# Where three small setup pieces stand among the first LSTM cells

## The chip, the core and the metric

The kernel runs on one core of a Trainium2 chip. The metric is device time in microseconds, from the launch's start to its end, as the median of several runs. Profiles come from one profiled execution: TensorE is PE (its weight loads PEld), VectorE is DVE, ScalarE is ACT, GpSimd is POOL, and SP issues DMAs. Each engine works through its own instruction list in order; semaphores tie the lists together.

## The reference

The input is `x` (16 batches, 512 nodes, 128 features) and an adjacency matrix of 512 x 512. Four graph layers follow one another, each with a residual sum and a layer norm:

```python
x = _layernorm(x + L0(x, adj))   # graph convolutions, order 2
x = _layernorm(x + L1(x, adj))   # normalized adjacency, two linear maps with batch norm
x = _layernorm(x + L2(x, adj))   # two graph convolutions, then LSTMs over windows of 1 to 4 nodes
x = _layernorm(x + L3(x, adj))   # 8 Euler steps of a diffusion
```

L3 is, for `t` in 8 steps,

```python
h = h + dt * (alph * 0.5 * (adj @ h - h) + h @ w_eff - h + x0)
```

Because it is linear in `h` and `x0`, the kernel writes the 8 steps as a polynomial: powers of the node matrix times powers of the feature matrix, plus a constant (`euler_bias`) that comes from the bias `fc_in_b` and needs to be made only once.

## The kernel before

The first half of the program (L0 and L1) ends at about 190 us. The second half handles L2 and L3 for 8 groups of two batches each. It is software-pipelined: in step `g` the engines run the 11 LSTM cells of group `g`, the front of L2 (turn, gather, weight) for group `g + 1`, and L3 of groups `g - 1` and `g - 2`.

The order is written out by hand. For each engine there is a table with one list for each of the 11 cells; `step` issues cell `c` and then the pieces that list `c` names (line 1252 and on). The cells are, by index: 0 and 1 the windows of one node (one for each batch), 2 and 3 the windows of two nodes (first and second time step), 4 to 6 those of three, 7 to 10 those of four. A cell on TensorE is the input matmuls (`wih`, three for each gate) and, from the second time step on, the recurrent ones (`whh`, L1860, L1861 and L1864), which wait for the state that VectorE writes. While the state is being made (ScalarE's gates L1433, VectorE's products L1585 to L1606, ScalarE's tanh L1436), TensorE works on the pieces of the list. The state of one cell group is the input of the next: cell 2 waits for the outputs of cells 0 and 1.

The first step (`ONCE_` tables) and the second (`NEXT_` tables) also carry the setup of L3, once. Three pieces of it matter here; all lead to `euler_bias`:

- `offset` (L2052): nine matmuls with 6 columns of weights into PSUM, then VectorE's copy (L1819) to `bc`. It needs the last of `fc` (`f_kept`).
- `lift`: twelve matmuls of the third power with 6 columns of weights (through the helper at L141 to L143, `pow_h,vpad_h`), eight small ones (L2063, L2064), then ScalarE's copy (L1557) to `vec_t`. It needs the low part of the last `second` piece (`p_lo`, VectorE L1748).
- `bias` (L2072): four matmuls of both, over 6 rows, then VectorE's copy (L1823) to `euler_bias`. L3's first transpose `x3t_0` (L1921) waits for that copy in the second step, since it uses the same PSUM banks.

Other names that occur: `gather0` and `gather1` are the products with the adjacency (`adj_h,node_h`), followed by ScalarE's cast (L1488) and VectorE's low part (L1643); `weight0` (L1900) and `weight1` (`gat_h,wg_parts`) use these; `hlate` (L2003) transposes the LSTM's result of the step before; `turn_0` (L1876) transposes the next group's input; `mix_0` to `mix_7` (L1810) are VectorE's sums for the coefficients of L3; the suffix is the batch of the pair. Every fp32 operand is kept as a high and a low part (`_h`, `_l`), which makes three matmuls of each product.

Of the kernel before, what the change touches and what calls it, by code (L numbers as in the profile page):

```python
# [54 lines left out]
def program(nc, x_t, adj_n, adj_t, nv1_t, nv2, l0_w, l0_b, w1_t, bn1, w2_t, bn2, wg, bg0, bg1,  # L55
# [4 lines left out]
    with ExitStack() as whole:  # L60
# [3 lines left out]
        def sb(name, shape, dt=F32):  # L64
# [25 lines left out]
                   w1_t, bn1, w2_t, bn2, eye, wg, wih_t, whh_t, bih, bhh, adj_h, adj_l, wih_h, wih_l, whh_h, whh_l,  # L90
                   wg_h, wg_l, gate_bias, row_sums, x1_dram, o2_dram, raw, xt, x1, small, small_in, steps)
        second_half(nc, sem, psum, wg_parts, banks, ident, exponent, scale2, shift2, adj_h, adj_l, wih_h, wih_l, whh_h, whh_l,
                    wg_h, wg_l, gate_bias, row_sums, x1_dram, o2_dram, x2_dram, raw, xt, x1, small, steps, out)

# [845 lines left out]
def second_half(nc, sem, psum, wg_parts, banks, ident, exponent, scale2, shift2, adj_h, adj_l, wih_h, wih_l, whh_h, whh_l,  # L940
# [8 lines left out]
    with ExitStack() as ctx:  # L949
# [215 lines left out]
        def outputs(c, source, ones, twos):  # L1165
# [9 lines left out]
            if p == 3:  # L1175
# [11 lines left out]
        FILL_ACT = [[], ["x3norm_0", "x3split_0", "evens_h"], ["x3t_0", "norm_0"],  # L1187
                    ["power1_0", "power2_0", "evens_l", "out_0", "gather0_0"], ["rest_h", "coefs0_0", "prep_1", "weight0_0", "x3norm_1"],
                    ["coefs1_0", "x3split_1", "rest_l"], ["gather1_0", "x3t_1", "norm_1"], ["power1_1", "out_1", "power2_1"],
                    ["input_0", "gather0_1"], ["weight0_1", "coefs0_1"],  # L1190
                    ["coefs1_1", "gather1_1", "ahead_0", "inner_0", "input_1", "inner_1"]]
# [38 lines left out]
        START_SP = ["norm_0", "norm_1"]  # L1230

        ONCE_PE = [[], ["turn_0", "first_3", "square"], ["cube", "second_0"], ["gather0_0", "fourth", "second_1"],
                   ["weight0_0", "fc_0"], ["turn_1", "fc_1"], ["gather1_0", "fc_2", "second_2"], ["weight1_0"],
                   ["gather0_1"], ["weight0_1", "second_3"], ["gather1_1", "offset", "weight1_1"]]
        ONCE_ACT = [["prep_0"], ["first_3"], ["norm_0", "evens_h", "second_0"], ["evens_l", "gather0_0", "second_1"],
                    ["rest_h", "prep_1", "weight0_0"], ["rest_l"], ["gather1_0", "second_2"], ["norm_1"],
                    ["input_0", "gather0_1"], ["weight0_1", "second_3"], ["gather1_1", "ahead_0", "input_1"]]
        ONCE_DVE = [[], ["turn_0", "first_3", "square"], ["cube", "second_0"], ["gather0_0", "fourth", "second_1"],
                    ["weight0_0", "fc_0"], ["turn_1", "fc_1"], ["gather1_0", "fc_2", "second_2", "mix_0"],
                    ["weight1_0", "mix_1"], ["gather0_1", "input_0", "mix_2"], ["weight0_1", "second_3", "mix_3"],  # L1240
                    ["gather1_1", "offset", "weight1_1", "input_1", "x3add", "x3first"]]
        ONCE_POOL = [[], ["turn_0"], ["norm_0"], [], [], ["turn_1"], ["norm_1"], [], [], [], ["whole", "x3first"]]
        ONCE_SP = [["prep_0", "prep_1"], [], ["norm_0"], [], ["ahead_0"], [], ["norm_1"], [], [], [], ["x3load"]]

        NEXT_PE = [["hlate"], ["lift", "turn_0", "bias"], ["x3t_0", "power1a_0"], ["power1b_0", "power2_0", "gather0_0"],
                   ["weight0_0", "coefs0_0"], ["coefs1_0", "turn_1"]] + FILL_PE[6:]
        NEXT_ACT = [[], ["lift"] + FILL_ACT[1], FILL_ACT[2] + ["split_e"], ["power1_0", "power2_0", "evens_l", "gather0_0"],
                    ["rest_h", "prep_1", "weight0_0", "coefs0_0", "x3norm_1"],
                    ["coefs1_0", "x3split_1", "rest_l"]] + FILL_ACT[6:]
        NEXT_DVE = [[], ["turn_0", "mix_4", "bias", "mix_5"], ["mix_6", "mix_7", "x3t_0", "x3sum_1"],  # L1250
                    ["power1_0", "power2_0", "gather0_0"], ["weight0_0", "coefs0_0"], ["coefs1_0", "turn_1"]] + FILL_DVE[6:]
        NEXT_POOL = FILL_POOL[:2] + [["norm_0", "split_e", "x3sum_1"]] + FILL_POOL[3:]

# [167 lines left out]
        def _(act):  # L1421
# [129 lines left out]
            def high(k, t):  # L1551
                act.wait_ge(p_done, NT * k + t + 1)
                nc.scalar.copy(pow_h[k + 1][:, t, :], product_bank(k, t)[:]).then_inc(p_hi, 1)
# [5 lines left out]
            def split_e():  # L1559
# [10 lines left out]
                            "first": lambda t: high(0, t), "second": lambda t: high(1, t),  # L1570
                            "input": layer_input}, START_ACT, ONCE_ACT, NEXT_ACT, FILL_ACT, LAST_ACT, TAIL_ACT)

        @block.vector
        def _(dve):
# [171 lines left out]
            def low(k, t):  # L1746
                dve.wait_ge(p_hi, NT * k + t + 1)
                nc.vector.tensor_tensor(pow_l[k + 1][:, t, :], product_bank(k, t)[:], f32(pow_h[k + 1][:, t, :]),  # L1748
                                        ALU.subtract).then_inc(p_lo, 1)
# [71 lines left out]
            def bias():  # L1821
# [10 lines left out]
                            "fourth": fourth, "fc": fc, "mix": mix, "offset": offset, "bias": bias, "first": lambda t: low(0, t), "second": lambda t: low(1, t),  # L1832
                            "input": layer_input}, START_DVE, ONCE_DVE, NEXT_DVE, FILL_DVE, LAST_DVE, TAIL_DVE)

        @block.tensor
        def _(pe):
# [231 lines left out]
            def bias():  # L2068
                pe.wait_ge(vt_kept, 1)
                pe.wait_ge(bc_kept, 1)  # L2070
                for t in range(NT):
# [11 lines left out]
                            "square": square, "cube": cube, "fourth": fourth, "fc": fc, "offset": offset, "lift": lift, "bias": bias},  # L2083
                START_PE, ONCE_PE, NEXT_PE, FILL_PE, LAST_PE, TAIL_PE)

# [51 lines left out]
```

## Time and profile before

| | us |
|---|---|
| median of 3 runs | 922.88 |
| lowest, highest | 922.36, 925.52 |
| profiled execution, its own time | 921.94 |
| span of its instructions | 920.1 |
| PE busy | 886.2 (96%) |
| PEld busy | 768.7 (84%) |
| DVE busy | 663.5 (72%) |
| ACT busy | 565.0 (61%) |
| POOL busy | 340.5 (37%) |

A row of a timeline gives the start and the busy time in us, then engine, line and operation with its output and inputs, and in brackets the idle time before it and what ended it. Matmuls overlap, so a matmul's pitch (start to next start) is shorter than its own duration. The chain of work that ended last runs over PE for 52% of the span. The first step of the second half begins at about 216 us, the second at about 289 us.

### The profile page before, as it was taken

How to read it: one execution, taken by the hardware profiler on the slowest of the kernel's cores; microseconds unless marked ns; L12 is line 12 of the kernel's file. 1: busy time of each engine (PE TensorE's matmuls, PEld its weight loads, DVE VectorE, ACT ScalarE, POOL GpSimd, SP SyncE). 2: the span in 40 equal slices, each digit the busy share in tenths (PEclk: the TensorE clock that was granted, in tenths of full speed). 3: DMA queues.
4: the chain of work that ended last, by engine and by line, in shares of the span. 5: the costliest groups of instructions: out<-in, count | busy, mean ns of one | idle time of the engine just before them, and what ended most of it. 6: DMA issues, size and time to landing. Idle time of an engine off the chain costs nothing.

```text
span 920.1 us, 14508 instructions
## 1 busy us (share of the span) xinstructions
PE 886.2 (96%) x4970; PEld 768.7 (84%) x4970; DVE 663.5 (72%) x1574; ACT 565.0 (61%) x1234; POOL 340.5 (37%) x548
## 2 busy tenths in 40 slices
PE   9999998988989999999999999999999999999996
PEld 6888985466877799888989898898989899978986
DVE  6988886876687866677677667767676777665744
ACT  6576756934755774677378547745763775466341
POOL 3768775630122520352153136214421631340221
PEclk9999999999999999999999999999999999999999
DMA  5422201320110101012001201010120001001000
GB/s 188 150 69 69 69 24 66 141 69 1 34 59 0 35 12 47 1 47 62 8 13 35 70 1 36 24 58 1 47 69 1 12 12 47 1 11 36 1 24 23
DMA packets 26594, 38.54 MB, mean 42 GB/s; under 512 B 3333, under 2 KB 12422, under 8 KB 26010
## 3 DMA queue, kind: packets, MB, share of 16 engines
q1 hardware_dynamic: 26088, 36.05, 11.8%
q10 hardware_dynamic: 434, 1.57, 0.5%
q8 instruction: 39, 0.64, 0.3%
q14 instruction: 33, 0.27, 0.1%
HBM read 21.89 MB, written 15.73 MB: 41 GB/s over the span
## 4 chain that ended last, share of the span: by engine, by line
PE 52%; DVE 11%; ACT 6%; POOL 6%; issue 4%; ACTq 0%; DVEq 0%; POOLq 0%
PE psum L141 15%; PE psum L143 14%; PE psum L142 14%; PE psum L1860 2%; PE psum L1864 2%; PE psum L1861 2%; ACT gate L1433 1%; POOL out_rstd L1366 1%; POOL node_l L1384 1%; DVE x L1634 1%; DVE x_stats L1612 1%; DVE in_h L1602 1%; POOL x_rstd L1366 1%; ACT raw L1464 1%; PE psum L1900 1%
## 5 line engine op out<-in xcount | busy, mean ns | idle before, releaser
L1433 ACT ACTIVATE gate<-psum,gate_bias 128x256 f32<-128x256 f32 (+2 forms) x296 | 143.7, 556 | 61.6 <-PE psum L1864 50.9
L141 PE MATMUL psum<-in_h,wih_h 128*128 128x256 f32 (+2 forms) x312 | 107.6, 345 | 7.5 <-DVE in_l L1606 5.0
L143 PE MATMUL psum<-in_h,wih_l 128*128 128x256 f32 (+2 forms) x312 | 104.1, 334 | 0.0
L142 PE MATMUL psum<-in_l,wih_h 128*128 128x256 f32 (+2 forms) x312 | 103.6, 332 | 0.0
L1400 POOL TENSOR_TENSOR gate<-in_h,in_l 128x512 f32<-128x512 f32 x14 | 17.9, 1306 | 157.5 <-DVE in_l L1606 157.5
L141 PEld LDWEIGHTS psum<-in_h,wih_h 128*128 128x128 f32 x312 | 59.2, 190 | 19.4 <-DVE in_l L1606 9.0
L1436 ACT ACTIVATE gate<-cell 128x512 f32<-128x512 f32 (+2 forms) x80 | 40.3, 503 | 50.7 <-DVE cell L1590 39.9
L1587 DVE TENSOR_TENSOR gate<-gate 128x256 f32<-128x256 f32 (+2 forms) x48 | 24.2, 504 | 59.4 <-ACT gate L1433 59.3
L142 PEld LDWEIGHTS psum<-in_l,wih_h 128*128 128x128 f32 x312 | 59.5, 191 | 5.5 <-issue 0.5
L143 PEld LDWEIGHTS psum<-in_h,wih_l 128*128 128x128 f32 x312 | 59.3, 190 | 4.8
L141 PE MATMUL psum<-e_h,shared 128*128 128x384 f32 x180 | 61.4, 341 | 0.2
L143 PE MATMUL psum<-e_h,shared 128*128 128x384 f32 x180 | 60.6, 336 | 0.0
L142 PE MATMUL psum<-e_l,shared 128*128 128x384 f32 x180 | 60.5, 336 | 0.0
L141 PE MATMUL psum<-shared 128*128 128x512 f32 x140 | 56.4, 403 | 2.3 <-DVE shared L729 1.6
L1860 PE MATMUL psum<-st_h,whh_h 128*128 128x256 f32 (+2 forms) x192 | 56.8, 314 | 1.2 <-DVE st_h L1595 1.2
L1861 PE MATMUL psum<-st_h,whh_l 128*128 128x256 f32 (+2 forms) x192 | 56.6, 313 | 0.0
L1358 POOL TENSOR_TENSOR x_mv<-x_stats 128x4 f32<-128x4 f32 x28 | 9.1, 324 | 127.2 <-DVE x_stats L1612 127.2
L1393 POOL TENSOR_TENSOR shared<-raw,shared 128x512 fp32r<-128x512 f32 x14 | 18.2, 1300 | 102.1 <-ACT shared L1503 102.1
L143 PE MATMUL psum<-shared 128*128 128x512 f32 x140 | 54.8, 391 | 0.0
L142 PE MATMUL psum<-shared 128*128 128x512 f32 x140 | 54.6, 390 | 0.0
L689 DVE SCALAR_TENSOR_TENSOR mix<-psum,coef,mix 128x256 f32<-128x256 f32 x96 | 46.4, 483 | 9.0 <-ACT mix L491 6.5
L141 PE MATMUL psum<-adj_h,node_h 128*128 128x512 f32 x120 | 47.6, 397 | 2.6 <-POOL node_l L1384 2.6
(395 smaller groups left out, 2887.4 us busy)
## 6 DMA issues: line engine op xcount, KB each, us to landing
x_spill<-x SPq DMA_DIRECT2D x30, 256.0 KB, 2.0
xt<-in_x_t_dram SPq DMA_DIRECT2D x16, 256.0 KB, 2.8
raw<-x_spill SPq DMA_DIRECT2D x16, 256.0 KB, 2.9
o_spill<-xt SPq DMA_DIRECT2D x14, 256.0 KB, 2.0
xt<-o_spill SPq DMA_DIRECT2D x14, 256.0 KB, 3.4
x<-x_spill SPq DMA_DIRECT2D x14, 256.0 KB, 3.5
out_dram<-raw SPq DMA_DIRECT2D x14, 256.0 KB, 2.3
raw<-in_adj_t_dram ACTq DMA_DIRECT2D x1, 1024.0 KB, 8.8
```

What stands on the lines that cost most here:

```text
L141: pe.matmul(dst, lh, rh, start=start, stop=False, **kw)
L142: pe.matmul(dst, lh, rl, start=False, stop=False, **kw)
L143: return pe.matmul(dst, ll, rh, start=False, stop=stop, **kw)
L689: chain.link(nc.vector.scalar_tensor_tensor(out=m, in0=scaled_block(t, k), scalar=coef[:, k - 1, t:t + 1], in1=m, op0=ALU.mult, op1=ALU.add))
L1366: chain.link(nc.gpsimd.tensor_tensor(rstd, rstd, exponent[:, 0:rstd.shape[-1]], ALU.pow))
L1393: nc.gpsimd.tensor_tensor(low[:], x3[:, j, :, :], f32(high[:]), ALU.subtract).then_inc(x3_lo, 1)
L1433: nc.scalar.activation(gate[q][:, 0:n], banks[GATE_BANK[q]][:, 0:n], ACT.Tanh if q == 2 else ACT.Sigmoid, bias=gate_bias[:, p - 1, q:q + 1 ...
L1436: nc.scalar.activation(gate[2][:, 0:n], cell[:, 0:n], ACT.Tanh).then_inc(tanh_ready, 1)
L1587: nc.vector.tensor_tensor(gate[0][:, 0:n], gate[0][:, 0:n], gate[2][:, 0:n], ALU.mult)
L1860: pe.matmul(bank, tile(whh_h[:, p - 2, :], q), st_h[:, 0:n], start=False, stop=False)
L1861: pe.matmul(bank, tile(whh_l[:, p - 2, :], q), st_h[:, 0:n], start=False, stop=False)
L1864: pe.matmul(banks[GATE_BANK[q]][:, 0:n], tile(whh_h[:, p - 2, :], q), st_l[:, 0:n], start=False, stop=True).then_inc(gate_sum, 1)
```

## The change

Only the tables of the order change; no instruction is added or removed. On TensorE and VectorE `offset` moves from the last list of the first step to list 7, behind `weight1_0`. `lift` moves from the second step's list 1 to the first step's last list, on TensorE ahead of `gather1_1`, and on ScalarE with its copy ahead of that gather's cast. In the second step's list 1, `bias` now stands ahead of `turn_0`, on VectorE ahead of `mix_4` too.

```diff
         ONCE_PE = [[], ["turn_0", "first_3", "square"], ["cube", "second_0"], ["gather0_0", "fourth", "second_1"],
-                   ["weight0_0", "fc_0"], ["turn_1", "fc_1"], ["gather1_0", "fc_2", "second_2"], ["weight1_0"],
-                   ["gather0_1"], ["weight0_1", "second_3"], ["gather1_1", "offset", "weight1_1"]]
+                   ["weight0_0", "fc_0"], ["turn_1", "fc_1"], ["gather1_0", "fc_2", "second_2"], ["weight1_0", "offset"],
+                   ["gather0_1"], ["weight0_1", "second_3"], ["lift", "gather1_1", "weight1_1"]]
...
-        NEXT_PE = [["hlate"], ["lift", "turn_0", "bias"], ["x3t_0", "power1a_0"], ["power1b_0", "power2_0", "gather0_0"],
+        NEXT_PE = [["hlate"], ["bias", "turn_0"], ["x3t_0", "power1a_0"], ["power1b_0", "power2_0", "gather0_0"],
...
-        NEXT_DVE = [[], ["turn_0", "mix_4", "bias", "mix_5"], ["mix_6", "mix_7", "x3t_0", "x3sum_1"],
+        NEXT_DVE = [[], ["bias", "turn_0", "mix_4", "mix_5"], ["mix_6", "mix_7", "x3t_0", "x3sum_1"],
```

The ScalarE and VectorE tables of the first step change in the same way.

On TensorE in list 7 of the first step, the difference between the two, from the end of `weight1_0` to the input matmuls of cell 8:

```order
 L142 MATMUL psum<-gat_l,wg_parts 128x512
 L143 MATMUL psum<-gat_h,wg_parts 128x512
+L2052 MATMUL psum<-bp,bcols 6x128 x9
 L141 MATMUL psum<-in_h,wih_h 128x256
 L142 MATMUL psum<-in_l,wih_h 128x256
```

`offset` comes in ahead of cell 8. Before, on TensorE at the end of the first step, from the end of `gather1_1` to cell 0 of the second step:

```order
L142 MATMUL psum<-adj_l,node_h 128x512
L143 MATMUL psum<-adj_h,node_l 128x512
L2052 MATMUL psum<-bp,bcols 6x128 x9
L141 MATMUL psum<-gat_h,wg_parts 128x512
L142 MATMUL psum<-gat_l,wg_parts 128x512
L143 MATMUL psum<-gat_h,wg_parts 128x512
L141 MATMUL psum<-in_h,wih_h 128x512
```

Now, at the same place:

```order
L142 MATMUL psum<-adj_l,node_h 128x512
L143 MATMUL psum<-adj_h,node_l 128x512
L141 MATMUL psum<-gat_h,wg_parts 128x512
L142 MATMUL psum<-gat_l,wg_parts 128x512
L143 MATMUL psum<-gat_h,wg_parts 128x512
L141 MATMUL psum<-in_h,wih_h 128x512
```

Nothing stands between the gather and the matmuls that use its cast any more; the lift's twenty matmuls stand ahead of the gather instead. Before, on TensorE behind cell 1 of the second step (the end of `lift`, `turn_0`, `bias`, cell 2):

```order
L2063 MATMUL psum<-ident_r,vpad_h 6x128
L2064 MATMUL psum<-ident_r,vpad_l 6x128
L1876 MATMUL psum<-ident,xt 128x128 x4
L2072 MATMUL psum<-raw 128x256 x4
L141 MATMUL psum<-in_h,wih_h 128x512
```

Now, behind cell 1's last matmuls:

```order
L142 MATMUL psum<-in_l,wih_h 128x512
L143 MATMUL psum<-in_h,wih_l 128x512
L2072 MATMUL psum<-raw 128x256 x4
L1876 MATMUL psum<-ident,xt 128x128 x4
L141 MATMUL psum<-in_h,wih_h 128x512
```

Between cells 1 and 2 the lift is gone, and `bias` and `turn_0` have changed places.

## Rows read from the trace of the kernel before

**Rows 1.** Stretches: us; busy of PE, PEld, DVE, ACT, POOL; clock; DMA share, GB/s

```profile
310.30:560.00 249.70, 248.96 (x1494) 225.12 (x1493) 177.10 (x389) 156.91 (x348) 83.05 (x158) 1.00 0.09 30
560.00:858.00 298.00, 292.70 (x1747) 265.04 (x1747) 207.71 (x466) 188.60 (x431) 92.80 (x181) 1.00 0.09 27
```

**Rows 2.** Timeline of TensorE around cell 8 of the first step

```profile
268.06 0.38 PE L1860 MATMUL psum<-st_h,whh_h 128*128 128x256 f32 x1 [1.18 <-DVE st_h L1595]
...
269.12 0.64 PE L1864 MATMUL psum<-st_l,whh_h 128*128 128x256 f32 x4
271.25 0.50 PE L141 MATMUL psum<-adj_h,node_h 128*128 128x512 f32 x1 [1.49 <-POOL node_l L1384]
```

**Rows 3.** Timelines of VectorE and GpSimd there

```profile
269.38 2.57 DVE L1810 SCALAR_TENSOR_TENSOR e<-bp,e 128x128 f32<-128x128 f32 x7
271.98 0.42 DVE L1587 TENSOR_TENSOR gate<-gate 128x256 f32<-128x256 f32 x1
...
269.82 1.37 POOL L1384 TENSOR_TENSOR node_l<-x,node_h 128x512 fp32r<-128x512 f32 x1 [7.68 <-ACT node_h L1483]
```

**Rows 4.** Timeline of TensorE at the end of the first step

```profile
283.62 0.45 PE L141 MATMUL psum<-adj_h,node_h 128*128 128x512 f32 x1
...
286.24 0.40 PE L143 MATMUL psum<-adj_h,node_l 128*128 128x512 f32 x1
286.56 2.13 PE L2052 MATMUL psum<-bp,bcols 128*6 128x128 f32 x18
288.73 0.50 PE L141 MATMUL psum<-gat_h,wg_parts 128*128 128x512 f32 x1
```

**Rows 5.** Timelines of VectorE and ScalarE, end of the first and of the second step

```profile
283.43 0.68 DVE L1748 TENSOR_TENSOR pow_l<-psum,pow_h 128x512 fp32r<-128x512 f32 x1
...
369.95 0.69 DVE L1643 TENSOR_TENSOR gat_l<-psum,gat_h 128x512 fp32r<-128x512 f32 x1 [2.22 <-ACT gat_h L1488]
...
369.33 0.58 ACT L1488 CAST gat_h<-psum 128x512 fp32r<-128x512 f32 x1 [2.53 <-PE psum L143]
```

**Rows 6.** Timeline of TensorE, second step, from `lift` to the mark

```profile
294.58 0.40 PE L141 MATMUL psum<-pow_h,vpad_h 128*6 128x512 f32 x1
...
297.83 0.60 PE L1876 MATMUL psum<-ident,xt 128*128 128x128 f32 x4
299.50 1.99 PE L2072 MATMUL psum<-raw 6*128 6x256 f32 x8 [1.07 <-ACT raw L1557]
301.42 0.50 PE L141 MATMUL psum<-in_h,wih_h 128*128 128x512 f32 x1
...
304.48 0.63 PE L143 MATMUL psum<-in_h,wih_l 128*128 128x512 f32 x1
305.63 0.63 PE L1921 MATMUL psum<-ident,raw 128*128 128x128 f32 x4 [0.52 <-DVE euler_bias L1823]
...
310.29 0.39 PE L1860 MATMUL psum<-st_h,whh_h 128*128 128x512 f32 x1
```

**Rows 7.** Timeline of VectorE, second step

```profile
300.35 0.69 DVE L1606 TENSOR_TENSOR in_l<-gate,in_h 128x512 fp32r<-128x512 f32 x1
...
304.26 1.23 DVE L1823 COPY euler_bias<-psum 128x1024 f32<-128x1024 f32 x1
...
307.51 0.69 DVE L1595 TENSOR_TENSOR st_h<-gate 128x512 fp32r<-128x512 f32 x1 [0.70 <-ACT gate L1436]
```

**Rows 8.** Stretches, TensorE alone: us, busy (matmuls), granted clock, DMA share, GB/s

```profile
213.40:216.80 3.40, 1.64 (x6) 0.99 0.00 0
216.80:220.10 3.30, 3.27 (x8) 0.50 0.00 0
268.06:271.25 3.19, 1.70 (x13) 1.00 0.40 107
298.40:301.40 3.00, 1.93 (x9) 1.00 0.02 5
301.40:305.60 4.20, 3.71 (x10) 0.59 0.00 0
```

More of the change, by code:

```diff
@@ L1235, in second_half @@
         ONCE_ACT = [["prep_0"], ["first_3"], ["norm_0", "evens_h", "second_0"], ["evens_l", "gather0_0", "second_1"],
                     ["rest_h", "prep_1", "weight0_0"], ["rest_l"], ["gather1_0", "second_2"], ["norm_1"],
-                    ["input_0", "gather0_1"], ["weight0_1", "second_3"], ["gather1_1", "ahead_0", "input_1"]]
+                    ["input_0", "gather0_1"], ["weight0_1", "second_3"], ["lift", "gather1_1", "ahead_0", "input_1"]]
         ONCE_DVE = [[], ["turn_0", "first_3", "square"], ["cube", "second_0"], ["gather0_0", "fourth", "second_1"],
@@ L1239, in second_half @@
                     ["weight0_0", "fc_0"], ["turn_1", "fc_1"], ["gather1_0", "fc_2", "second_2", "mix_0"],
-                    ["weight1_0", "mix_1"], ["gather0_1", "input_0", "mix_2"], ["weight0_1", "second_3", "mix_3"],
-                    ["gather1_1", "offset", "weight1_1", "input_1", "x3add", "x3first"]]
+                    ["weight1_0", "offset", "mix_1"], ["gather0_1", "input_0", "mix_2"], ["weight0_1", "second_3", "mix_3"],
+                    ["gather1_1", "weight1_1", "input_1", "x3add", "x3first"]]
@@ L1242, in second_half @@
         ONCE_POOL = [[], ["turn_0"], ["norm_0"], [], [], ["turn_1"], ["norm_1"], [], [], [], ["whole", "x3first"]]
         ONCE_SP = [["prep_0", "prep_1"], [], ["norm_0"], [], ["ahead_0"], [], ["norm_1"], [], [], [], ["x3load"]]
-        NEXT_PE = [["hlate"], ["lift", "turn_0", "bias"], ["x3t_0", "power1a_0"], ["power1b_0", "power2_0", "gather0_0"],
+        NEXT_PE = [["hlate"], ["bias", "turn_0"], ["x3t_0", "power1a_0"], ["power1b_0", "power2_0", "gather0_0"],
                    ["weight0_0", "coefs0_0"], ["coefs1_0", "turn_1"]] + FILL_PE[6:]
-        NEXT_ACT = [[], ["lift"] + FILL_ACT[1], FILL_ACT[2] + ["split_e"], ["power1_0", "power2_0", "evens_l", "gather0_0"],
+        NEXT_ACT = [[], FILL_ACT[1], FILL_ACT[2] + ["split_e"], ["power1_0", "power2_0", "evens_l", "gather0_0"],
```

## Prediction

> **What bounds the kernel now.** First I read the page's busy shares and then the stretches of the trace with TensorE's busy time. From 310.3 us on TensorE is busy 248.96 of 249.7 us and 292.70 of 298 us [rows 1]. So in the steady steps TensorE's queue is the bound, and whatever delays it before 310 us is carried to the end. The later waits follow TensorE's own results, so a shift is not given back there. The question is only how much later or earlier TensorE reaches that part. As the mark I take the recurrent matmuls of the second step's first two-step cell, at 310.29 [rows 6].
>
> Next I read TensorE's timeline with what ended each wait. The change touches four waits:
> - at cell 8 of the first step, 1.18 us for `st_h`, to 268.06 [rows 2];
> - before `gather0_1`, 1.49 us for GpSimd's `node_l`, to 271.25 [rows 2];
> - before `bias` in the second step, 1.07 us for the lift's copy (`raw`, L1557), to 299.50 [rows 6];
> - before `x3t_0`, 0.52 us for the `euler_bias` copy, to 305.63 [rows 6].
>
> Last, the granted clock. It is 1.00 (2.4 GHz) nearly everywhere, and at its half level (1.2 GHz) in two places: 216.8 to 220.1, behind a stretch in which TensorE was busy 1.64 of 3.4 us, and from about 302 us, behind the wait and the matmuls over 6 rows of `bias` [rows 8].
>
> **Part 1: `offset`, three lists forward.** It is 18 passes in 2.13 us [rows 4]. It now stands ahead of cell 8, whose input matmuls end at 266.88 (268.06 less 1.18). With it they end at 269.0, and the recurrent ones start 0.95 us late. They and the low parts take 1.7 us (268.06 to 269.76, that is 271.25 less 1.49), so TensorE is done at about 270.7. `node_l`, which comes from the first cell list's norm through ScalarE and GpSimd, is still ready at 271.25 [rows 2, 3]. So the 2.13 us disappear in 2.67 us of idle time. Queued behind the later cell 8 are its gates and VectorE. VectorE gets `offset`'s copy of 256 columns (about 0.4 us, like its product L1587 of as many [rows 3]) ahead of `mix_1`. Today `mix_1` ends just as cell 8's first product starts at 271.98 [rows 3], so that cell is late by about 0.4 us. There is no wait on TensorE at cells 9 and 10, so this is cost 0. The bounds are 0 and +0.4. The fourth list's `second_3` then still ends where it did, and cell 10's matmuls give way to the next piece at 283.62 as before [rows 4].
>
> **Part 2: the first step's end.** `lift` needs the low part of `second_3`, which VectorE writes from 283.43 in 0.68 us, to 284.11 [rows 5]. TensorE waits there about 0.55 us, where today it went straight on with `gather1_1`. Then come the 12 wide and 8 narrow matmuls of `lift`, 294.58 to 297.83, 3.25 us [rows 6], and the gather, 2.86 us (last matmul at 286.24, the first at 283.62) [rows 4]. Behind the gather stand ScalarE's cast and VectorE's low part. In the second step, where both engines are free, the cast runs 369.33 to 369.95 and the low part 0.69 us more [rows 5]. The last matmul (0.40 us [rows 4]), 0.62, 0.69 and 0.09 us of signalling make 1.80 us from its start to `weight1_1`, of which 0.23 us is its own pitch (2.86 us over 12 matmuls, rounded down). So 1.57 us of idle time stand open where `offset` and a gap of 0.1 us lay. `weight1_1` starts at 283.62 + 0.55 + 3.25 + 2.86 + 1.57 = 291.85, against 288.73 [rows 4]: **+3.1 us**. Low bound +2.5 (no wait for `p_lo`, copies as fast as their busy times), high bound +3.6 (the late VectorE work of part 1 lies on it). I take 3.1, since each term is a row of the same operation.
>
> The lift's copy on ScalarE (0.56 us) stands ahead of the cast, but its input is ready 2.9 us earlier: cost 0.
>
> **Part 3: from `weight1_1` to cell 2 of the second step.** Today TensorE fills this with cells 0 and 1, `hlate`, `lift`, `turn_0` and `bias`, until 301.42. But cell 2 also needs cell 1's outputs, the last row of VectorE's chain (L1606), from 300.35 in 0.69 us, to 301.04 [rows 7]. That chain starts with `hlate` and cell 0, behind `weight1_1`, and nothing in it was shortened. So cell 2 may start 12.3 to 12.4 us behind `weight1_1`, against 12.7 today: about 304.2, **+2.8 us**. The 3.25 us of `lift` were cover for a wait that the chain sets anyway. What is left there is `bias` (1.92 us, 299.50 to 301.42) and `turn_0` (0.6). Cell 1 ends at 297.7, TensorE is through at 300.3, and then sits idle for **3.9 us**, the longest wait of the middle of the kernel.
>
> **Part 4: behind cell 2.** Today from cell 2's start to `x3t_0` 4.21 us pass (301.42 to 305.63): nine matmuls, most at 0.43 us pitch at the half clock, and then the wait for `euler_bias`, which VectorE writes from 304.26 in 1.23 us [rows 6, 7]. So today's slow clock costs nothing of its own: `euler_bias` came last. Now `bias` precedes `turn_0` on both engines, the copy is done at about 305.4, and `x3t_0` follows cell 2 directly. At the full clock nine matmuls take 2.1 us, which gives back 2.1 us: the shift would be +0.7. From `x3t_0` to the mark are 4.66 us. VectorE's `st_h` for the mark (307.51 + 0.69 today [rows 7], 3.1 us later now) would be at 311.3, so the floor is **+1.0 us**.
>
> **Part 5: the clock.** The trace shows a fall behind 3 us with 1.07 us idle and 1.93 us of mostly 6-row matmuls, and behind 3.4 us with 1.64 us busy; it shows none in 3.19 us with 1.70 busy [rows 8]. A stretch of 300.3 to 304.2 with nothing, and only `bias` and a transpose ahead of it, is far emptier than either that fell. I therefore expect cell 2 to begin at the half clock again, and now nothing hides it. Both low stretches of the trace lasted about 3.4 us: 216.8 to 220.1 at 0.50, and 4.2 us at a mean of 0.59, which is 3.4 us at half (4.2 x 0.41 x 2) [rows 8]. A microsecond there does half of its work. A low stretch of 3.4 us costs 1.7 us. Bounds: 0 (if no fall), and 3.4 us (all 6.7 us of work up to the mark done half in a stretch twice as long). I take 1.7, the row of the same length.
> The Trainium skill bears on this ("TensorE: Matmul & The Clock Gate", section "Why this matters for your kernels"): it warns of idle gaps between bursts of matmuls, since the clock then drops to half. By that rule the move that opens the gap pays twice, once for the wait and once behind it; if the clock stayed up, the sum would stand at its floor. The two low stretches agree with it.
>
> **The sum.** +2.8 (cell 2's start) − 2.1 (cell 2 to `x3t_0` at the full clock) + 1.7 (clock) = **+2.4 us**. The profiled execution took 921.94 us (span 920.1 and 1.84 around it), so its like would take 924.3. The median of the three runs is 922.88, 0.94 above the profiled one; I put the forecast at 922.88 + 2.3 = **925.2 us**. A measurement of this kernel can tell about 0.3%, 2.8 us, from no change; 2.3 is just inside.
>
> **Rivals.**
> - *The clock falls earlier or stays low longer* (the rival on the slower side). The place is `weight1_1`: from 288.4 to 291.85 TensorE would be busy 1.9 of 3.4 us, between the stretch that fell and the one that didn't [rows 8]. If it falls there, `weight1_1` and cell 0 run 12 matmuls at 0.43 instead of 0.233 us, +2.3 us, and the chain of part 3 starts that much later. The same price comes from a low stretch behind cell 2 that lasts past 6 us. Either gives 925.2 + 2.0 = 927.2. It decides from a wait there of about 1.8 us, the idle time that lay before the first fall (3.40 less 1.64). For it: 1.57 is only 0.2 us short of that. Against: 1.5 us of idle time left the clock at 1.00 [rows 8], and the new waits of 0.55 and 1.57 us lie 6 us apart.
> - *The clock stays up or its price is hidden*: the floor, +1.0 and below, 923.8. For it: it costs nothing today. Against: part 5.
> - *TensorE's work is only moved*: same matmuls, a bound engine, and the 2.67 us won at cells 8 and 9 pay for the new waits; 922.9. Against it: the four waits of before sum to 4.3 us and the new ones to 0.5 + 0.55 + 1.57 + 3.9 = 6.5.
> - *It gains*: the chain of part 3 isn't what holds cell 2, which starts right behind `turn_0`. Then 3.9 us and the clock's price fall off: 925.2 − 5.6 = 919.6. For it: the chain ended only 0.4 us ahead of TensorE, so it was never seen to hold it alone. Against: the semaphore is there, and TensorE's weight load waited for L1606 at this place.
>
> **How the numbers follow.** Forecast 0.48 (its own range 923.9 to 926.6), clock lower for longer 0.22, clock up 0.13, only moved 0.12, gain 0.05. Slower by over 0.3% (above 925.65) is the second case and a third of the first: 0.38. Faster by over 0.3% (below 920.1) is the last: 0.05. The rest is 0.57. The range of 8 in 10 leaves out the gain and the upper part of the slow case: 922.5 to 927.4.
>
> **What would show it.** Cell 8 without a wait and one of about 0.5 us before `gather0_1`; `lift` at about 284.2; `weight1_1` at about 291.9 with 1.6 us of wait before it; cell 2 at about 304.2 behind 3.9 us of wait for L1606; no wait before `x3t_0`; half clock in cell 2. I am wrong if cell 2 starts before 303, if the clock stays at 1.00 there, or if it falls between 288 and 296.

## The result and the profile after

The change makes the kernel slower by about 4 us. Run side by side with the kernel before, it took 927.63 us in the median of 14 runs (925.23 to 929.68), the kernel before 923.35 (921.29 to 925.58, 14 runs): a ratio of 1.0042, 95% interval 1.0031 to 1.0053, that is +2.9 to +4.9 us. Two later comparisons, on two chips, gave 1.0032 [1.0018, 1.0047] and 1.0039 [1.0025, 1.0053]. The forecast was +2.3 us, at 925.2, with a range of 922.5 to 927.4. The measured median lies 0.2 us above that range; but the kernel before was itself 0.47 us slower here than in the three runs from which the forecast started, and by the ratio (926.8 on those 922.88) the result is inside. The profiled execution took 929.68 us (span 927.9), the longest of the 14.

Timeline of TensorE after the change, from `offset` in list 7 to the mark:

```profile
265.26 2.13 PE L2052 MATMUL psum<-bp,bcols 128*6 128x128 f32 x18
...
268.86 0.28 PE L1860 MATMUL psum<-st_h,whh_h 128*128 128x256 f32 x1
...
272.25 0.50 PE L141 MATMUL psum<-adj_h,node_h 128*128 128x512 f32 x1 [1.79 <-POOL node_l L1384]
...
285.17 0.40 PE L141 MATMUL psum<-pow_h,vpad_h 128*6 128x512 f32 x1 [0.39 <-DVE pow_l L1748]
...
292.85 0.50 PE L141 MATMUL psum<-gat_h,wg_parts 128*128 128x512 f32 x1 [1.40 <-DVE gat_l L1643]
...
298.80 1.99 PE L2072 MATMUL psum<-raw 6*128 6x256 f32 x8
300.72 0.66 PE L1876 MATMUL psum<-ident,xt 128*128 128x128 f32 x4
305.20 0.80 PE L141 MATMUL psum<-in_h,wih_h 128*128 128x512 f32 x1 [3.83 <-DVE in_l L1606]
...
309.21 0.61 PE L1921 MATMUL psum<-ident,raw 128*128 128x128 f32 x4
...
313.86 0.39 PE L1860 MATMUL psum<-st_h,whh_h 128*128 128x512 f32 x1
```

Cell 8's wait [rows 2] is gone. The wait before `gather0_1` is 1.79 us long and ends 1.0 us later than in before [rows 2], where none of it was forecast. The rest has the places and nearly the sizes of the forecast: 0.39 us for `pow_l`, 1.40 for `gat_l`, 3.83 for `in_l` (forecast 0.55, 1.57 and 3.9), no wait before `x3t_0`.

VectorE and GpSimd at cell 8, after:

```profile
269.25 0.41 DVE L1819 COPY raw<-psum 6x256 f32<-6x256 f32 x1
269.58 1.49 DVE L1810 SCALAR_TENSOR_TENSOR e<-bp,e 128x128 f32<-128x128 f32 x7
271.14 1.33 DVE L1587 TENSOR_TENSOR gate<-gate 128x256 f32<-128x256 f32 x1
...
269.69 2.50 POOL L1384 TENSOR_TENSOR node_l<-x,node_h 128x512 fp32r<-128x512 f32 x1 [7.72 <-ACT node_h L1483]
```

In before GpSimd's `node_l` took 1.37 us and VectorE's seven sums of `mix_1` 2.57 [rows 3]. Now `node_l` takes 2.50, the sums 1.49, and the product behind them 1.33 instead of 0.42. The two engines still work at the same time, but who is stretched has changed: this time it is `node_l`, for which TensorE waits. The durations of the single sums (shortest, median and longest in ns), before and after, say how:

```profile
L1810 DVE SCALAR_TENSOR_TENSOR e<-bp,e x7: 279/282/1352, 269.4 to 271.7; 128x128 f32<-128x128 f32 x7
L1810 DVE SCALAR_TENSOR_TENSOR e<-bp,e x7: 269/273/274, 269.6 to 270.8; 128x128 f32<-128x128 f32 x7
```

In before one single sum stood still until `node_l` was done. In after none did; `node_l` took 1.13 us longer beside them, and then the product stood still.

Stretches of TensorE after (us, busy, granted clock, DMA share, GB/s):

```profile
292.85:301.38 8.53, 8.52 (x41) 1.00 0.01 2
301.40:305.20 3.80, 0.00 (x0) 0.63 0.00 0
305.20:309.20 4.00, 4.00 (x9) 0.50 0.00 0
309.20:313.86 4.66, 4.66 (x24) 1.00 0.00 0
```

All of cell 2 runs at the half clock, as forecast, behind 3.8 us with no matmul. Before it the clock is whole, so it does not fall at `weight1_1`. The mean of 0.63 over the 3.80 us of the wait says that the fall came 2.8 us before cell 2 (3.80 x 0.37 x 2): the low stretch lasted 6.8 us in all, not the forecast's 3.4, and 2.8 of them lay in the wait.

The executions differ by a common offset from the first half. So I count from the first `fc` matmul (L2047), which the change doesn't touch (247.40 us in before, 247.24 in after). "Cell 4" is the first of cell 4's input matmuls. Shifts against before, in us, from each kernel's timeline:

| profiled execution | `gather0_1` | `weight1_1` | cell 2 | `x3t_0` | mark | cell 4 |
|---|---|---|---|---|---|---|
| forecast | 0 | +3.1 | +2.8 | +2.4 | +2.4 | +2.4 |
| the change, three executions | +1.1 to 1.2 | +4.2 to 4.3 | +3.9 | +3.7 | +3.7 to 3.8 | +4.0 |
| before, a second execution | 0 | 0 | 0 | 0 | 0 | 0 |
| copy_behind, two executions | 0 | +3.1 | +2.8 | +2.6 | +3.1, +3.4 | +3.1, +3.3 |
| lift_alone | 0 | +3.7 | +3.4 | +3.7 | +3.9 | +3.9 |
| offset_alone | +1.1 | +2.7 | +3.4 | +3.2 | +3.8 | +3.8 |
| after_awake | +1.1 | +4.2 | +3.9 | +1.9 | +1.9 | +5.1 |
| awake_turn | +1.1 | +5.8 | +5.5 | +4.0 | +4.0 | +5.5 |
| bias_first | 0 | 0 | +1.2 | +0.9 | +1.5 | +1.5 |
| lift_split | 0 | 0 | 0 | −0.8 | −0.5 | −0.3 |
| before_nudge | 0 | 0 | 0 | −1.8 | −1.8 | −0.3 |

### The profile page after: what moved, and what is told of

Its sections match the earlier page's. It is cut to its first block, busy times and chain, and to the rows that moved or that the text cites. A ratio compares the mean times of both kernels' runs of the same rounds, so it can differ in the third digit from the quotient of the medians.

```text
span 927.9 us, 14507 instructions
## 1 busy us (share of the span) xinstructions
PE 889.3 (96%) x4970; PEld 771.0 (83%) x4970; DVE 662.7 (71%) x1574; ACT 565.7 (61%) x1234; POOL 343.7 (37%) x548
## 3 DMA queue, kind: packets, MB, share of 16 engines
q10 hardware_dynamic: 434, 1.57, 0.5%
## 4 chain that ended last, share of the span: by engine, by line
PE 53%; DVE 11%; ACT 6%; POOL 5%; issue 4%; ACTq 0%; DVEq 0%; POOLq 0%
PE psum L141 15%; PE psum L143 15%; PE psum L142 15%; PE psum L1861 2%; PE psum L1860 2%; PE psum L1864 2%; ACT gate L1433 2%; ACT raw L1464 1%; DVE in_h L1602 1%; ACT gate L1436 1%; POOL node_l L1384 1%; DVE gate L1587 1%; DVE cell L1590 1%; PE psum L1900 1%; DVE in_l L1606 1%
## 5 line engine op out<-in xcount | busy, mean ns | idle before, releaser
L1433 ACT ACTIVATE gate<-psum,gate_bias 128x256 f32<-128x256 f32 (+2 forms) x296 | 144.2, 557 | 63.3 <-PE psum L1864 51.7
L1587 DVE TENSOR_TENSOR gate<-gate 128x256 f32<-128x256 f32 (+2 forms) x48 | 25.7, 536 | 60.9 <-ACT gate L1433 60.7
```

Source lines behind the costliest of these rows:

```text
L1433: nc.scalar.activation(gate[q][:, 0:n], banks[GATE_BANK[q]][:, 0:n], ACT.Tanh if q == 2 else ACT.Sigmoid, bias=gate_bias[:, p - 1, q:q + 1 ...
L1587: nc.vector.tensor_tensor(gate[0][:, 0:n], gate[0][:, 0:n], gate[2][:, 0:n], ALU.mult)
```

## The experiments

**The change again (after_again, after_third).** No edit; each ran side by side with a group of the variants below.

> The changed kernel once more, in the same company. Theory (a shift of 3.6 to 4.0 us up to the mark is all that the change makes, and the rest of the profiled execution's +7.8 us is its clock's phase and GpSimd's): +3.5 to +4.5 us against before, the same collision in list 7, and the later +0.5 us a step and the low clock at 828 us may be absent. Rival (the later loss belongs to the change): both are there again and the time is +6 us or more.

> The change unaltered, as the company of the kernel above. Theory A: 927.0 us or so, +3.5 to +4 against before, and within 1 us of that at any mean clock but for 1.8 us for each 0.002 of mean clock. Theory B (the difference from before is the clock alone): at the same mean clock the change is within 1 us of before.

Measured: 927.07 us (12 runs, ratio 1.0032) and 925.96 (6 runs, 1.0039 [1.0025, 1.0053]). Both profiles repeat the wait of 1.79 us with `node_l` at 2.50 us, and every shift up to cell 4 within 0.1 us. Most of what the first profile lost behind cell 4 (its span is +7.8 us in all) does not come back: after_again's span is 925.0, after_third's 923.8. Part of it does. From cell 4 to the long wait at about 821 us, before took 501.05 us and its second profile 501.12; the change took 503.41, 501.77 and 502.23, and copy_behind (below) 501.40 and 501.35. Most of this is a wait that neither profile of before shows there, four times in after, once in after_again and twice in after_third (the second time 0.16 us), like this one of after:

```profile
507.75 0.89 PE L1864 MATMUL psum<-st_l,whh_h 128*128 128x340 f32 x4 [0.54 <-DVE st_l L1597]
```

So the loss grows by 0.7 to 2.4 us behind cell 4, differently in each execution. It is not shown whether the change makes this more frequent: offset_alone has three such waits and lift_alone one, the others without extra matmuls none.

**One half of the change each.** Only `offset` to list 7 (offset_alone); only `lift` ahead of `gather1_1`, with `offset` where it was and `turn_0` ahead of `bias` on TensorE (lift_alone).

```diff
 offset_alone
-... ["weight1_0"], ... ["gather1_1", "offset", "weight1_1"]]
+... ["weight1_0", "offset"], ... ["gather1_1", "weight1_1"]]
 lift_alone
-... ["gather1_1", "offset", "weight1_1"]]   NEXT: ["lift", "turn_0", "bias"]
+... ["lift", "gather1_1", "offset", "weight1_1"]]   NEXT: ["turn_0", "bias"]
```

These and the diffs below are shortened. NEXT is the second step's list 1; the tables of the engines that copy the results change with TensorE's.

> Only `offset` moves (list 7 of the first step, its copy ahead of `mix_1`); `lift` and the order of `bias` stay as before. Theory (each part acts by itself): cell 8's wait goes, `gather0_1` starts about 1.0 us late because GpSimd's `node_l` meets VectorE's `mix_1` and cell 8 and takes 2.5 instead of 1.4 us; `weight1_1` then waits 1.4 us where `offset` took 2.1, so it starts at +0.2 to +0.3 us, and the time is that of before within 0.5 us. Rival (the collision is chance of one execution, not of the order): `node_l` takes 1.3 us, `weight1_1` starts 0.8 us early, 0.8 us faster.

> Only `lift` moves (ahead of `gather1_1`, its copy too); `offset` stays between the gather and `weight1_1`, `turn_0` ahead of `bias`. Theory (the lift was free cover between cells 1 and 2): `weight1_1` at +3.8 us (3.25 and 0.55 of wait), no wait of its own; cell 2 behind 3.9 us of wait at +3.5; half clock there; +3.0 to +4.5 us in the time. Rival (the lift's new place is harmless, the loss is all GpSimd's collision in list 7): within 1 us of before.

Measured: offset_alone 924.26 us (12 runs), 1.0006 [0.9988, 1.0024]; lift_alone 926.27 (12 runs), 1.0027 [1.0016, 1.0039]. By the times most of the loss is the lift's move: its profile shows the forecast's rows (`weight1_1` at +3.7, cell 2 behind 3.98 us of wait), though its time, +2.5 us by the ratio, is under the expected +3.0 to +4.5; the rival's 1 us is outside its interval. The interval of offset_alone (−1.1 to +2.2 us) can't tell whether its loss at `gather0_1` reaches the end. Its profiled execution stands higher than its median (+3.8 at the mark). The half clock fell in it twice: behind the wait at `gather0_1` (1.5 us) and ahead of cell 2, in `bias` (2.74 us instead of 1.99). The two halves' profiles tell more than their times. `node_l` takes 2.50 us wherever `offset`'s copy precedes `mix_1`, and 1.37 where it doesn't. And taking `offset` out from behind the gather gains nothing there, which TensorE's wait in offset_alone shows:

```profile
290.00 0.50 PE L141 MATMUL psum<-gat_h,wg_parts 128*128 128x512 f32 x1 [2.10 <-DVE gat_l L1643]
```

Its wait of 2.10 us has the length of the 2.13 us of `offset` that it replaces [rows 4]. VectorE in offset_alone shows why it is more than the 1.57 that I had worked out: the products of cell 10 stand ahead of `gat_l`, without a gap.

```profile
288.13 0.43 DVE L1602 TENSOR_TENSOR in_h<-gate 128x256 fp32r<-128x256 f32 x1 [0.48 <-ACT gate L1436]
...
288.92 0.42 DVE L1606 TENSOR_TENSOR in_l<-gate,in_h 128x256 fp32r<-128x256 f32 x1
289.27 0.68 DVE L1643 TENSOR_TENSOR gat_l<-psum,gat_h 128x512 fp32r<-128x512 f32 x1
```

With the lift ahead of the gather that chain has ended in time, and 1.40 us remain. `offset` had been free cover.

**VectorE's order alone (copy_behind, copy_behind_2).** The change, with `mix_1` ahead of `offset`'s copy.

```diff
-                    ["weight1_0", "offset", "mix_1"], ["gather0_1", ...
+                    ["weight1_0", "mix_1", "offset"], ["gather0_1", ...
```

> The change as made, but VectorE runs mix_1 ahead of offset's copy. Theory A (the copy ahead of mix_1 moved mix_1 beside GpSimd's node_l, L1384, which then took 2.50 us instead of 1.37): node_l is back at about 1.4 us, gather0_1 starts at the time of before (271.2, less any common offset of the run), weight1_1 comes +3.1 us against before instead of +4.1, the mark +2.7 instead of +3.7, and the time is about 1 us below the change's, a ratio to before of about 1.003. Theory B (cell 8's later gates, not VectorE's order, made the collision): node_l stays at 2.5 us and nothing moves.

> Once more the change with VectorE's mix_1 ahead of offset's copy, beside the change itself on the same chip. Theory A (the 1.1 us that the collision at cell 8 adds are carried to the end): the mean of the runs that have the same mean granted clock lies 1 to 2 us below the change's, and the medians differ by about 1 us unless this kernel falls into a further half-clock stretch near the end (before the wait for in_l at about 842 us) more often. Theory B (a microsecond at cell 8 is absorbed later): at the same mean clock the two kernels take the same time within 0.5 us.

Timeline of TensorE, then VectorE and GpSimd, in copy_behind_2:

```profile
269.33 0.50 PE L141 MATMUL psum<-adj_h,node_h 128*128 128x512 f32 x1 [0.67 <-POOL node_l L1384]
...
289.91 0.50 PE L141 MATMUL psum<-gat_h,wg_parts 128*128 128x512 f32 x1 [1.40 <-DVE gat_l L1643]
...
302.25 0.79 PE L141 MATMUL psum<-in_h,wih_h 128*128 128x512 f32 x1 [3.82 <-DVE in_l L1606]
```

```profile
267.45 2.58 DVE L1810 SCALAR_TENSOR_TENSOR e<-bp,e 128x128 f32<-128x128 f32 x7
270.06 0.41 DVE L1819 COPY raw<-psum 6x256 f32<-6x256 f32 x1
...
267.90 1.37 POOL L1384 TENSOR_TENSOR node_l<-x,node_h 128x512 fp32r<-128x512 f32 x1 [7.71 <-ACT node_h L1483]
```

`node_l` is back at 1.37 us and the sums at 2.58. `gather0_1` waits 0.67 us, and the shifts are +3.1 at `weight1_1`, +2.8 at cell 2 and +2.6 at `x3t_0`: the forecast's own numbers within 0.2 us. In time it is less plain: 926.52 us (5 runs, 1.0038 [1.0026, 1.0050]) and 925.36 (8 runs, 1.0033 [1.0021, 1.0045]), against 925.96 for the change beside the second of them. The expected 1 us lies within the intervals, so it is not shown by the medians. Each run also carries its mean granted clock. At 0.992 the change's runs have a mean of 927.33 us (21 runs), copy_behind's 925.28 (9 runs): 2 us less at the same clock, and 1.8 us on the chip that ran both (927.16, 3 runs, against 925.32, 7 runs), as Theory A of copy_behind_2 said. That is more than the 1.1 us of the collision; the waits for `st_l`, which neither profile of copy_behind has, would make up the rest. But 4 of copy_behind's 13 runs have 0.990, only 3 of the change's 32. Part of the gain may thus be paid back in clock, in the way that before_look shows below.

**The clock held up (after_awake, awake_turn).** Sixteen extra matmuls of 512 columns (results unused) in the wait ahead of cell 2; in awake_turn also `turn_0` ahead of `bias` on both engines.

```diff
+            def awake():
+                for _ in range(16):
+                    pe.matmul(banks[2][:], tile(adj_h[:, 0, :], 0), adj_h[:, 0, :], start=True, stop=True)
-                    ["bias", "turn_0"]
+                    ["bias", "turn_0", "awake"]      awake_turn: ["turn_0", "bias", "awake"]
```

> The changed kernel with 16 matmuls of 512 columns behind `turn_0`, whose result nobody reads, so that TensorE isn't idle before cell 2. Theory (half clock behind the empty gap costs TensorE about 1.7 us): granted clock 1.00 in cell 2, which starts at the same place (the wait for L1606 is the bound), the mark 1.2 to 1.9 us earlier than in the changed kernel, and the time by as much. Rival (the price of the clock is hidden by VectorE): clock 1.00, but the mark within 0.3 us of the changed kernel's.

> The change with 16 extra 512-column matmuls in the long wait ahead of cell 2 (their results are not used), and with turn_0 ahead of bias again on TensorE and VectorE. Theory A (with bias first, turn_0's copy and statistics on VectorE start 1.2 us later, and the norm chain through GpSimd and ScalarE ahead of cell 3's gates becomes the next bound, which is why the higher clock alone bought nothing): VectorE's L1634 starts at about 305.1 instead of 306.2, the wait of 3.1 us before cell 4 shrinks to 2 us or less, the clock stays at 1.00 there or falls later, and the time is 1 to 2 us below the change's (ratio to before about 1.002 to 1.003). Theory B (the clock's 1.7 us are lost again whatever the order, since the stretched product L1587 beside GpSimd sets cell 4): the wait before cell 4 stays at about 3 us and the ratio at about 1.004 to 1.005.

Measured: 928.78 us (9 runs), 1.0050 [1.0032, 1.0068]; and 927.73 (5 runs), 1.0051 [1.0039, 1.0063]. In after_awake the clock is 1.00 in cell 2, `x3t_0` comes 1.8 us earlier than in after and the mark 1.9 us. Thirteen microseconds on it is all lost, and more, and the clock falls there instead (mean 0.62 from 325.5 to 330.0). TensorE there:

```profile
325.50 0.42 PE L141 MATMUL psum<-in_h,wih_h 128*128 128x340 f32 x1 [3.09 <-DVE in_l L1606]
```

Cell 4 waits 3.09 us for cell 3's outputs. On ScalarE the norm of the next group's input stands in the queue ahead of cell 3's gates (L1433):

```profile
313.73 1.65 ACT L1464 ACTIVATE x<-x,x_shift,x_rstd 128x128 f32<-128x128 f32 x4 [2.08 <-POOL x_shift L1367]
315.41 0.62 ACT L1483 CAST node_h<-x 128x512 fp32r<-128x512 f32 x1
315.94 1.16 ACT L1561 CAST e_h<-e 128x1152 fp32r<-128x1152 f32 x1
316.99 0.68 ACT L1433 ACTIVATE gate<-psum,gate_bias 128x512 f32<-128x512 f32 x1
```

GpSimd's `x_shift` sets the start, and its chain begins with VectorE's copy of `turn_0` (L1634), which cell 1 holds back. The product L1587 then meets GpSimd and takes 2.31 us (0.83 in before). So the clock's price is real where it falls, and in this kernel its return bought nothing at the end. In awake_turn the half clock fell behind the 1.78 us wait at `gather0_1` (mean clock 0.67 from 272.1 to 276.0), and everything came 1.6 us later. So its shifts are best counted from `weight1_1`: L1634 started 12.21 us behind it (13.36 in after_awake), and cell 4 31.08 us (32.22), behind a wait of 1.40 us. The order did what Theory A said of the rows, 1.1 us; that the time is Theory B's goes with the earlier fall, so the time doesn't decide between the two.

**The order of `bias` and `turn_0` alone (bias_first).**

```diff
-["lift", "turn_0", "bias"]     DVE: ["turn_0", "mix_4", "bias", "mix_5"]
+["lift", "bias", "turn_0"]     DVE: ["bias", "turn_0", "mix_4", "mix_5"]
```

> Before with one edit: in the second step's list 1 bias ahead of turn_0, on VectorE ahead of mix_4 too; offset and lift where they were. Theory A (the order alone is close to nothing on TensorE: the wait for lift's copy grows from 1.07 to about 1.7 us since turn_0 no longer covers it, but cell 2 follows turn_0 at nearly the same time; x3t_0's 0.52 us wait goes): cell 2 within 0.3 us of 301.4, the mark within 0.7 us, ratio 0.999 to 1.001. Theory B (turn_0 and the norm chain behind it are what the next cells wait for): VectorE's L1634 comes about 2.5 us later than in before (300.96), a new wait of 1 us or more stands before cell 4, and the ratio is 1.001 to 1.003.

Measured: 923.03 us (11 runs), 1.0004 [0.9994, 1.0014]. Cell 2 came at +1.2, since `turn_0` now stands between `bias` and cell 2 and the clock had fallen in `bias`: `bias` took 2.40 us instead of 1.99 and `turn_0` 1.11 instead of 0.60. The mark came at +1.5, outside what Theory A allowed; its time agrees with A. Theory B's wait before cell 4 didn't come. Neither holds as a whole.

**A version that should win (lift_split).** `offset` in list 7 with its copy behind `mix_1`; the lift's first six matmuls in the wait behind `gather1_1`, the rest at its old place; on VectorE `bias`'s copy right behind `turn_0`'s.

```diff
-... ["gather1_1", "offset", "weight1_1"]]   NEXT: ["lift", "turn_0", "bias"]
+... ["gather1_1", "lifta", "weight1_1"]]    NEXT: ["liftb", "turn_0", "bias"]
```

> A version that should beat both: offset in list 7 with its copy behind mix_1; of lift only the first six matmuls (1.4 us) stand in the first step, between gather1_1 and weight1_1, in the wait for the gather's low part; the other fourteen stay in the second step's list 1 ahead of turn_0 and bias, with ScalarE's copy at its old place; on VectorE bias's copy stands right behind turn_0's. My theory (the wait behind the gather is 1.57 us and is now filled; cell 2 follows weight1_1 at 12.3 us by the chain): weight1_1 at -0.6 us against before, cell 2 at -0.9, x3t_0 without a wait, the mark -1 to -2.5 depending on the clock, ratio 0.997 to 0.999. Rival (GpSimd and VectorE collide here too, or the half clock falls earlier because of the shorter work): the mark at +0.5 to +1.5, ratio 1.000 to 1.002.

Measured: 923.94 us (12 runs), 1.0020 [1.0010, 1.0030]: slower than before. `weight1_1` is at 0 and not at −0.6: the lift's 1.4 us and a wait of 0.71 us fill the same 2.1 us, up to the end of cell 10's chain. The 0.5 us won at the mark ended as 0.3 at cell 4, and the profiled execution lost 1.5 us to the clock near the end. None of its 12 runs has a mean clock above 0.992, and at 0.992 they have a mean of 923.90 us (9 runs), before's on the same chip 924.00 (8 runs): its loss goes with the clock.

**Before, looked at again, and with its clock held (before_look, before_nudge).** before_look has no edit.

```diff
 before_nudge
-["lift", "turn_0", "bias"]            DVE: ["turn_0", "mix_4", "bias", "mix_5"]
+["lift", "turn_0", "nudge", "bias"]   DVE: ["turn_0", "bias", "mix_4", "mix_5"]
```

> Before unaltered, for a second profile. The question is the stretch between the two long waits for in_l near the end (821.13 and 841.52 us in before's profile, 20.39 us apart, and 21.9 to 22.0 us apart where the clock fell there: in the change's profile, and in two variants that start there at 821.7 to 822.4). Theory A (it falls or not by where in time the same work lies, not by the kernel): before's second profile has 20.4 or 21.9 us, and the rows up to 310 us are those of the first within 0.3 us beside a common offset. Theory B (the change makes it fall): 20.4 us again.

> Before with five extra 512-column matmuls (1.2 us at the full clock, results not used) in the wait ahead of bias in the second step, and with bias's copy on VectorE right behind turn_0's, ahead of mix_4; offset and lift where they were. Theory A (before's cell 2 runs at the half clock because of that wait, and the late euler_bias only hides it): clock 1.00 in cell 2, bias within 0.3 us of where it was, x3t_0 1 to 2 us earlier and without a wait, the mark 1 to 2 us earlier, ratio 0.998 to 0.9995: a version ahead of both. Theory B (the matmuls over 6 rows are what lets the clock fall): half clock in cell 2 again, x3t_0 0.5 us earlier at most, ratio 1.000 to 1.002.

In before_look cell 2 ran at the full clock (1.00 from 300.18 to 304.40), unlike in the first profile [rows 8], and nothing came of it. TensorE waited longer for the same copy:

```profile
304.40 0.63 PE L1921 MATMUL psum<-ident,raw 128*128 128x128 f32 x4 [1.85 <-DVE euler_bias L1823]
...
309.05 0.39 PE L1860 MATMUL psum<-st_h,whh_h 128*128 128x512 f32 x1
```

All shifts up to cell 4 are 0.0. Theory A of before_look holds. Near the end it is the other way round. The stretch between the two long waits for `in_l`, in before and in before_look:

```profile
821.00:824.00 3.00, 2.87 (x17) 1.00 0.28 83
824.00:828.00 4.00, 4.00 (x27) 1.00 0.01 3
```

```profile
821.00:824.00 3.00, 3.00 (x11) 0.50 0.31 87
824.00:828.00 4.00, 4.00 (x25) 1.00 0.00 0
```

The same kernel fell there in one execution, 1.6 us, and not in the other. In the profiles it fell where the work behind the first wait began at 819.96, 821.24, 821.68, 822.28, 822.41, 822.82 and 827.32 us, and not at 821.13, 824.59, 824.81, 825.40, 826.04, 827.00 and 829.07. So a shift of a microsecond elsewhere can add 1.6 us here, whichever kernel it is. Both profiles of copy_behind fell there and one of the change's three, which would blur copy_behind's gain; how often it falls in the runs without a profile isn't shown.

before_nudge: 922.60 us (12 runs), 1.0003 [0.9994, 1.0012]. The clock stayed at 1.00, `x3t_0` and the mark came 1.8 us earlier as Theory A said, and the time didn't. TensorE shows where it went:

```profile
319.75 0.42 PE L141 MATMUL psum<-in_h,wih_h 128*128 128x340 f32 x1 [1.37 <-DVE in_l L1606]
```

Cell 4 came only 0.3 us earlier. What held it is the same pair of engines. Cell 3's first product (L1587) and GpSimd's `e_l`, in before and then in before_nudge:

```profile
313.95 0.83 DVE L1587 TENSOR_TENSOR gate<-gate 128x512 f32<-128x512 f32 x1 [2.30 <-ACT gate L1433]
311.54 2.68 POOL L1415 TENSOR_TENSOR e_l<-e,e_h 128x1152 fp32r<-128x1152 f32 x1
```

```profile
312.53 2.33 DVE L1587 TENSOR_TENSOR gate<-gate 128x512 f32<-128x512 f32 x1 [1.82 <-ACT gate L1433]
311.61 2.69 POOL L1415 TENSOR_TENSOR e_l<-e,e_h 128x1152 fp32r<-128x1152 f32 x1
```

The product started 1.4 us earlier and ended at the same time, 0.56 us behind the end of `e_l`. So it does in twelve of the fourteen profiles (0.54 to 0.56 us behind it, whether it takes 0.71 or 2.33 us); in lift_alone and offset_alone it starts as late as the end of `e_l` or later and takes 0.69. `e_l` stands behind the norm chain that begins with L1634, and L1634 came no earlier with the clock up (at 0.0 against before in before_nudge, within 0.05 us of after's place in after_awake). No variant beat the kernel before.

## Why the prediction was right or wrong

**The sign was right, the size was off by 1.6 us.** The step that failed is Part 1's cost 0, with its bounds 0 to +0.4. It kept `node_l` ready at 271.25 because nothing in its own chain had changed. But the copy ahead of `mix_1` moved VectorE's sums against GpSimd's `node_l`, which rose from 1.37 to 2.50 us: +1.1 to +1.2 at `gather0_1`. copy_behind takes just this away, and the shift there is 0. Half of the pair stood in before's own trace, where eight such sums, away from `node_l`, take less than the seven of [rows 3]:

```profile
264.95 1.70 DVE L1810 SCALAR_TENSOR_TENSOR e<-bp,e 128x128 f32<-128x128 f32 x8
```

I had read the long sums as their own duration.

**Part 2 was right.** From `gather0_1`'s shift on, +3.1 at `weight1_1` was forecast and +3.1 measured (copy_behind; in after 4.3 less 1.2). Waits of 0.39 and 1.40 us stood where 0.55 and 1.57 were forecast; the idle time by pitches is a little longer than what the rows print in brackets. What it left unsaid is that `offset`'s 2.13 us were cover for cell 10's chain; lift_alone, offset_alone and lift_split show it.

**Part 3 was right.** Cell 2 follows `weight1_1` by 12.35 us in after (forecast 12.3 to 12.4), behind 3.83 us for L1606, where the forecast said 3.9. In lift_alone, with `turn_0` first, it was 3.98: the lift's 3.25 us were cover for a chain, and their removal brought nothing.

**Part 4 was right on TensorE**: `x3t_0` follows cell 2 without a wait. That before's half clock costs nothing was only argued there, and is shown now by before_look (`x3t_0` and the mark at 0.0 with the clock at 1.00).

**Part 5 was right in kind and place, and its size almost.** The half clock covered all nine matmuls of cell 2: 4.01 us from cell 2 to `x3t_0`, against 2.2 in after_awake at the full clock, so a price of 1.8 us where 1.7 was forecast. That the sizes agree is partly luck: the price was worked out for a low stretch of 3.4 us that begins with cell 2, and the one that came lasted 6.8 us, began 2.8 us earlier and ended with cell 2. The Trainium skill's page "TensorE: Matmul & The Clock Gate", section "Why this matters for your kernels", warns that behind an idle gap between bursts of matmuls the clock is back at half. The trace agrees: 3.83 us of wait, and a granted clock of 0.50 behind it. But removing the clock's price gained nothing in the end, since cell 4 came at +5.1 in after_awake. So the rival with the clock up, 923.8, had a false floor: I worked the floor out at the mark and took it that a shift there is carried on. The losses here were carried on. A gain needs the next chain too: in before_nudge 1.8 us at the mark were 0.3 at cell 4, behind the product that waits for `e_l`.

**The sum.** With the missed 1.16 us the forecast of +2.4 at `x3t_0` becomes +3.6; measured +3.7. From the mark to cell 4 another 0.3 us came (cell 3's product L1587 took 1.35 to 1.51 us, 0.83 in before), and the time is +3.9, +3.0 and +3.6 by the three ratios. That this meets +4.0 at cell 4 is not the whole account: the change's profiles lose another 0.7 to 2.4 us between cell 4 and 821 us, which no term of the forecast has, and the fall at 821 us adds 1.6 us to some executions of either kernel. The forecast itself took 2.3 for a sum of 2.4, without a reason. Held at the same mean clock, the change's runs lie 3.0 us above before's at 0.994 (925.63, 6 runs, against 922.61, 39 runs) and 3.2 at 0.992 (927.33, 21 runs, against 924.12, 17 runs; 32 runs of the change and 74 of before in all, from several chips; before's first 14 have no clock on record). The rest of the 3.9 would be that its runs are less often at 0.994: 6 of 32 against 39 of 74. That cell 2 is slow in each of its profiles, and in one of before's two, goes with this and doesn't prove it.

What stays open: why one of VectorE's sums stands still when they start 0.44 to 0.45 us ahead of `node_l`, and `node_l` is the one stretched when they start 0.11 us ahead (so in all fourteen profiles; the copy just ahead of the sums goes with the second case, and no run separates the two); what brings the waits of 0.53 us for `st_l`; and what sets whether the clock falls at 821 us, beyond where in time the work lies.

## What to carry to other kernels

Before a piece is moved out from in front of a wait, look at what it covers: a piece between two links of another engine's chain costs nothing, and moving it to a busy place makes it cost its full length. Before a small copy is put ahead of VectorE's work, look at what GpSimd does at the new time, since an unchanged GpSimd operation can become 1.1 us longer. A gain counts only up to the next chain: follow the trace one wait further than the one removed, before it is added to the sum. Where a row of VectorE is long, look for a shorter one of the same operation elsewhere in the trace: the difference is a wait that the row does not name.

## What the runs showed of the hardware

- GpSimd and VectorE together: seven sums of two inputs took 2.57 to 2.58 us with `node_l` at 1.37 to 1.38 (eight profiles), or 1.48 to 1.49 with `node_l` at 2.49 to 2.50 (six profiles), and the product of 256 columns behind them 0.40 to 0.43 or 1.33. Who pays changed with a shift of 0.3 us between the two engines.
- The one that pays is not slowed evenly. One sum of seven took 1.35 us and the median one 0.28. And a product of 512 columns beside GpSimd's `e_l` ended 0.54 to 0.56 us behind it, wherever it had begun, in twelve profiles.
- The same wait of 1.8 us at `gather0_1`, with TensorE busy 1.5 to 1.7 of the 3.3 to 3.5 us ahead of its end, left the clock at 1.00 in the change's profiles, and was followed by the half clock in offset_alone and awake_turn (0.62 over 4.5 us, 0.67 over 3.9 us). A forecast for such a place is a chance, not a rule.
- The mean granted clock that comes with each run sorts the times of one kernel: before took 922.61 us at 0.994 and 924.12 at 0.992.
